# Unit 0's inverse roots on ScalarE and VectorE, its normalising ahead of the low weight parts, its first scores ahead of unit 1's projection

## The chip, the cores and the metric

The kernel runs on one core of a Trainium2 chip. The metric is the device time of one execution in microseconds. Five instruction streams run side by side and meet at semaphores only: TensorE (PE; its weight loads are PEld), VectorE (DVE), ScalarE (ACT), GpSimd (POOL) and the DMA queue of SyncE (SP). Each stream is executed in the order in which it is written: an instruction that waits holds back all that stand behind it on its engine.

## The reference

Four residual blocks on x of shape (4, 256, 256), each on a layer norm of x: a WKV recurrence with the context as values, a quantised dense layer with ReLU, a grouped-query attention with fp8 rounding (self attention and attention to the context), and a small linear attention. The change lies in the third, whose core is:

```
ln_out = _ln(hidden_states, ln_w, ln_b)
q  = _fp8_linear_pertensor(ln_out, wq,  wq_scale,  q_in_scale)   # 16 heads of 128
k  = _fp8_linear_pertensor(ln_out, wk,  wk_scale,  k_in_scale)   # 8 groups
v  = _fp8_linear_pertensor(ln_out, wv,  wv_scale,  v_in_scale)
qx = _fp8_linear_pertensor(ln_out, wqx, wqx_scale, qx_in_scale)
kx, vx = split(einsum('bsi,oi->bso', cond, w_kv_x))
q, k, qx, kx = _ln(...) of each, over its 128 columns
core = softmax(q k^T / sqrt(128)) v ;  xout = softmax(qx kx^T / sqrt(128)) vx
x = x + fp8(cat(core, xout) / smooth) @ wproj^T * scale
```

## The kernel before

The attention is cut into 32 units (`UNITS`): unit u is one group (two query heads) of one of the four batch rows, 256 rows in two halves t = 0, 1. For each unit `project` computes 1024 columns per half in float32 and bf16 parts into PSUM banks `QB[0..3]`; ScalarE takes the sums of squares (`squares`), GpSimd turns them into inverse roots `rs` by a power (`powers`), VectorE multiplies by them (`normalise`), PE transposes the result (`turn`), ScalarE evacuates it with the norm's weights (`evacuate`), PE computes a bf16 copy of the scores (`guard`), VectorE takes its row maxima `nm` (`maxima`), GpSimd spreads them on a diagonal `diag` (`diagonals`), and PE adds that diagonal to the scores (`scores`), of which ScalarE takes the exponentials (`exps`); `weigh` multiplies by the values. The weights of the eight groups are prepared once: for group g, PE turns four blocks (`weights(g, n)`), ScalarE writes their high part, VectorE the low one (`low_weights`), and GpSimd splits the remainder of the third block again (`narrow_parts`).

The order on each engine is written out by hand. The head of the kernel (the first 70 us) runs batch row 0 through the first two blocks and prepares the weights of groups 0 to 3; then a loop over the units sets a fixed order. The change lies at the end of the head, between the last fp8 step of batch row 0 (`fp8(0, (3,))`, VectorE) and the start of the loop. Lines in the trace: the low parts are L1703, the normalising L1720 and L1722, the transposes of `turn` L663, the `guard` L677, the maxima L1730, the diagonal L1332, the scores L691 and L692, the projections L591 and L598, the layer norm statistics L1460, L1463 and L1465, its application L1470, `narrow_parts` L1323 and L1325, the constants `cs` (cosines and sines for the last block, 32 one-column memsets) L1361 and L1362.

A bank of PSUM that PE wants to write again is guarded by `free(o)`, which waits for the bank's last reader. Two of them matter here. Bank XB (bank 7) holds first `turn_h(1)`, the transposed layer norm of batch row 1, which ScalarE's `turned_h(1)` (L999) reads, and then `weights(3, 3)`. Bank SB[0] (bank 4) holds first `weights(3, 0)`, read by `low_weights(3, 0)`, and then the first scores.

## Time and profile before

| quantity | us |
|---|---|
| median of 3 runs | 690.91 (690.83 to 692.33) |
| profiled execution, its own time | 692.9 |
| span of the profile, first to last instruction | 691.1 |
| TensorE busy | 617.9 (89% of the span) |
| VectorE busy | 530.1 (77%) |
| ScalarE busy | 401.0 (58%) |
| GpSimd busy | 254.0 (37%) |

The profile is one execution; its time lies 1.8 us above its span and 2.0 us above the median of the timed runs, so that differences are taken within it and then laid on the median. Starts are counted from the first instruction. In a timeline a row of several instructions (x4) gives the start of the first and the time until the last has ended; neighbouring instructions of one engine overlap a little at their ends. What stands in brackets is the idle time before the row and who ended it.

### The profile page before, as it was taken

The page shows a single profiled execution, that of the slowest core. Times are in us where ns is not written, and L with a number is a line of the kernel's source. Part 1 is how long each engine was busy: PE and PEld are TensorE (multiplying, and loading weights), DVE is VectorE, ACT ScalarE, POOL GpSimd, SP SyncE. Part 2 cuts the span into 40 slices and gives each one's busy share as a digit, 9 for nine tenths or more (in the row PEclk, how much of TensorE's full clock was granted, in tenths as well). Part 3 has the DMA queues.
Part 4 walks back from the last instruction along what each step waited for, and adds up shares of the span by engine and source line. Part 5 has one row for each costly group of instructions (what it writes and reads, how often), then busy time and mean ns, then how long its engine had stood idle before and what let it go on. Part 6 is the DMA issues. An engine that isn't in the chain of part 4 may idle for free.

```text
span 691.1 us, 13273 instructions
## 1 busy us (share of the span) xinstructions
PE 617.9 (89%) x4567; PEld 490.6 (71%) x4567; DVE 530.1 (77%) x1285; ACT 401.0 (58%) x1339; POOL 254.0 (37%) x338
## 2 busy tenths in 40 slices
PE   4446989999989999999899999999999999999936
PEld 3235767766767877877688778877788778877725
DVE  6997778979676757888787568797763776769698
ACT  4255756656777736556757365667563566653531
POOL 2215564444223543334235533332322254421233
PEclk9998999999999999999999999999999999999978
DMA  8236443443483223223243333223342223010001
GB/s 271 73 147 222 138 115 69 153 158 80 146 280 115 76 90 100 100 100 100 100 115 100 100 100 100 100 101 100 100 160 100 98 102 101 16 32 1 1 0 62
DMA packets 36972, 72.86 MB, mean 105 GB/s; under 512 B 3342, under 2 KB 28586, under 8 KB 32810
## 3 DMA queue, kind: packets, MB, share of 16 engines
q1 hardware_dynamic: 36720, 72.00, 32.4%
q8 instruction: 37, 0.61, 0.4%
q14 instruction: 29, 0.24, 0.1%
q10 hardware_dynamic: 186, 0.02, 0.0%
HBM read 59.41 MB, written 12.60 MB: 104 GB/s over the span
## 4 chain that ended last, share of the span: by engine, by line
PE 65%; DVE 22%; ACT 5%; issue 4%; POOL 2%; DMA 1%; SPq 0%; DVEq 0%; ACTq 0%
PE bank L711 14%; PE bank L591 12%; PE bank L691 11%; PE bank L598 7%; PE bank L663 5%; PE bank L735 3%; PE bank L677 3%; PE bank L692 3%; DVE Cb L1745 2%; PE bank L725 1%; POOL rs L1317 1%; PE bank L750 1%; PE bank L481 1%; DVE Cb L1760 1%; DVE rest L1703 1%
## 5 line engine op out<-in xcount | busy, mean ns | idle before, releaser
L711 PEld LDWEIGHTS bank<-V,Pt 128*128 128x128 f32 x1024 | 128.0, 192 | 37.5 <-DVE Cb L1745 26.1
L711 PE MATMUL bank<-V,Pt 128*128 128x129 f32 x1024 | 138.2, 278 | 9.4 <-DVE Cb L1745 9.3
L1069 ACT ACTIVATE square<-bank 128x128 bf16<-128x128 f32 x372 | 98.1, 275 | 78.4 <-PE bank L591 50.8
L1332 POOL TENSOR_TENSOR diag<-identb,nm 128x512 bf16<-128x512 bf16 x64 | 67.1, 1048 | 198.9 <-DVE nm L1730 198.8
L691 PE MATMUL bank<-QT,KTt 128*128 128x512 f32 x256 | 132.7, 600 | 2.4 <-POOL diag L1332 2.4
L1052 ACT ACTIVATE Pt<-bank 128x512 f32<-128x512 f32 x128 | 76.7, 599 | 77.6 <-PE bank L692 74.1
L1730 DVE TENSOR_REDUCE nm<-bank 128x2 f32<-128x512 f32 x128 | 82.0, 682 | 32.5 <-PE bank L677 32.4
L1317 POOL TENSOR_TENSOR rs<-ve,mhalf 128x6 f32<-128x6 f32 x64 | 88.9, 1389 | 5.3
L1743 DVE RECIPROCAL ro<-bank 128x2 f32<-128x2 f32 x128 | 21.3, 166 | 83.3 <-PE bank L711 82.7
L1745 DVE SCALAR_TENSOR_TENSOR Cb<-bank,ro,ism 128x128 bf16<-128x128 f32 x256 | 78.1, 347 | 4.5
L591 PE MATMUL bank<-WQ,xq 128*128 128x256 f32 x512 | 79.7, 298 | 1.8 <-DVE xq L1641 1.5
L591 PEld LDWEIGHTS bank<-WQ,xq 128*128 128x128 f32 x512 | 67.4, 189 | 14.0 <-issue 6.9
L1069 ACT ACTIVATION_READ_ACCUMULATOR square<-bank 128x1 f32 x372 | 76.0, 204 | 0.0
L598 PE MATMUL bank<-WC,vT 128*128 128x256 f32 x256 | 70.6, 400 | 0.0
L1315 POOL TENSOR_SCALAR ve<-ss 128x6 f32<-128x6 f32 x64 | 18.4, 288 | 128.6 <-ACT square L1069 128.6
L1093 ACT ACTIVATE QT<-bank,vec 128x512 f32<-128x512 f32 x64 | 49.9, 780 | 22.6 <-PE bank L663 22.5
L591 PE MATMUL bank<-WH,xh 128*128 128x128 bf16 x768 | 54.0, 220 | 1.5 <-DVE xh L1641 1.5
L691 PEld LDWEIGHTS bank<-QT,KTt 128*128 128x128 f32 x256 | 43.1, 190 | 17.1 <-issue 13.8
L1720 DVE TENSOR_TENSOR Qn<-bank,rs 128x512 f32<-128x512 f32 x64 | 43.8, 684 | 13.4 <-POOL rs L1317 13.4
L663 PE MATMUL bank<-ident,Qn 128*128 128x128 f32 x384 | 48.8, 278 | 2.4 <-DVE Qn L1722 2.4
L1101 ACT ACTIVATE catT<-bank 128x1024 bf16<-128x1024 bf16 x32 | 32.8, 1024 | 27.7 <-PE bank L725 27.7
L692 PE MATMUL bank<-diag,onesb 128*128 128x512 bf16 x128 | 48.5, 379 | 0.0
(233 smaller groups left out, 1030.7 us busy)
## 6 DMA issues: line engine op xcount, KB each, us to landing
WQ<-wq_split SPq DMA_DIRECT2D x24, 1024.0 KB, 7.8
WH<-wh_split SPq DMA_DIRECT2D x24, 384.0 KB, 9.0
wq_split<-WQ SPq DMA_DIRECT2D x8, 1024.0 KB, 4.4
ism<-smooth_inverse SPq DMA_DIRECT2D x32, 256.0 KB, 6.4
wst<-in_L_xattn_wproj SPq DMA_DIRECT2D x16, 256.0 KB, 4.0
wh_split<-WH SPq DMA_DIRECT2D x8, 384.0 KB, 3.8
wst<-in_L_xattn_wq SPq DMA_DIRECT2D x8, 256.0 KB, 5.2
wst<-in_L_xattn_wqx SPq DMA_DIRECT2D x8, 256.0 KB, 5.2
```

The lines of the kernel that those rows point to most:

```text
L591: last = nc.tensor.matmul(o[:, o0:o0 + n], x, w, start=m == 0, stop=m == parts * KT - 1)
L598: last = nc.tensor.matmul(QB[2 * t + 1][:, 2 * P:4 * P], vT[b % 2][:, k, t * P:(t + 1) * P], WC[:, k, g, :], start=k == 0, stop=k == KT - 1)
L663: last = nc.tensor.transpose(o[:, (j * NT + t) * P:(j * NT + t + 1) * P], Qn[:, t, h, :], ident[:])
L691: nc.tensor.matmul(o[:], KTt[u % 2][:, x, t * P:(t + 1) * P], QT[u % 2][:, x, :], start=True, stop=False)
L692: nc.tensor.matmul(o[:], onesb[:], diag[u % 2][:, x].rearrange("p a b -> p (a b)"), start=False, stop=True).then_inc(s["st_done"], 1)
L711: last = nc.tensor.matmul(o[:, h * (P + 2):h * (P + 2) + P + 1], Pt[:, x, k, h * S + t * P:h * S + (t + 1) * P], V[u % 2][:, x, k, 0:P + 1 ...
L1052: A(Pt[:, x, t], SB[n % 2][:], ACT.Exp, scale=SCALE).then_inc(s["exp_done"], 1)
L1069: last = A(square[:, t, h], head(t, h), ACT.Square, accum_out=ss[:, t, h:h + 1])
L1317: gp.tensor_tensor(rs[:, t, :], ve[:, t, :], mhalf[:, 0:6], ALU.pow).then_inc(s["rs_ready"], 1)
L1332: gp.tensor_tensor(diag[u % 2][:, x], identb[:].unsqueeze(1).to_broadcast([P, HPG * NT, P]), nm[u % 2][:, x].rearrange("p h t -> p (h t)") ...
L1730: v.tensor_reduce(nm[u % 2][:, x, :, t], GUARD_BANK[t][:].rearrange("p (h t) -> p h t", h=HPG), AX_X, ALU.max, negate=True).then_inc(s["ma ...
L1745: last = v.scalar_tensor_tensor(out=c4[:, t, x, h, :], in0=o[:, h * (P + 2):h * (P + 2) + P], scalar=ro[:, x, t, h:h + 1], in1=ism[:, u % ...
```

## The change

Five edits, all in the head:

1. The inverse roots of unit 0. Before, GpSimd computed them with `powers(0, 0)` and `powers(0, 1)`. Now ScalarE takes a square root (scale 1/128, bias EPS) over both halves at once behind its last square, and VectorE a reciprocal. Around it two one-element activations on a new tile `table` load ScalarE's function tables: one for the square root before `turned_z(0)`, one for the exponential behind the values. ScalarE's `values(0, 0)` moves ahead of the squares of the second half.
2. VectorE: reciprocal and `normalise(0, *)` move ahead of the three `low_weights(2, *)` and of batch row 1's layer norm statistics; `middle(1, 0)` (L1470, whose result `turn_h(1)` turns) moves behind all four maxima of unit 0.
3. TensorE: `turn(0)` moves ahead of `weights(3, 0)` and `weights(3, 1)`; the first scores of unit 0 move from the start of the loop to behind `guard(0, 1)`; `turn_h(1)` moves behind those scores.
4. ScalarE: the first exponentials move ahead of `weights(3, 2)`, and `turned_h(1)` behind it.
5. GpSimd: the 32 memsets of `cs` move ahead of `narrow_parts(1)`; `norm(1, 0)` moves behind `narrow_parts(2)`.

```diff
--- before.py
+++ after.py
@@ -93,6 +93,8 @@
         lnm = sb("lnm", [P, 3, NT, 2])
         lnst = sb("lnst", [P, NT, 6])
         mhalf = sb("mhalf", [P, 16])
+        epsb = sb("epsb", [P, 1])
+        table = sb("table", [P, 1])
         cs = sb("cs", [P, B, 2, DK3 // 2])
         st3 = sb("st3", [P, T8, 6])
         mv3 = sb("mv3", [P, T8, 2])
@@ -300,7 +302,7 @@
 
             "xq_ready xqT_done xqT_evac ffn_done ffn_read zT_done lnT_evac y4_ready xq4_ready "
 
-            "qkv_done q1_done v_ready ss_ready rs_ready norm_done tr_done qt_evac smax_done "
+            "qkv_done q1_done v_ready ss_ready root_ready rs_ready norm_done tr_done qt_evac smax_done "
             "max_ready diag_ready st_done exp_done pv_done o_evac cq_ready cT2_done catT_evac proj_done x3_ready "
 
             "ve3_ready pw3_ready h3_ready h3T_done h3T_evac conv_ready silu_ready proj3_done qkv3_evac rotated dl_ready "
@@ -775,13 +777,14 @@
             for n in range(3):
                 weights(2, n, HEAD_BANK[2][n])
             project_first()
+            turn(0)
             weights(3, 0, HEAD_BANK[3][0])
             weights(3, 1, HEAD_BANK[3][1])
-            turn(0)
-            turn_h(1)
             guard(0, 0)
             weights(3, 2, HEAD_BANK[3][2])
             guard(0, 1)
+            scores(0, 0, 0)
+            turn_h(1)
             weights(3, 3, HEAD_BANK[3][3])
             project(1, 0)
 
@@ -879,7 +882,8 @@
             for u in range(UNITS - 1):
                 b, g = divmod(u, G)
                 nb, step = ahead(u) or (None, None)
-                scores(u, 0, 0)
+                if u:
+                    scores(u, 0, 0)
                 if u >= SCORES_FIRST:
                     scores(u, 0, 1)
                 if (u + 1) % G == 0:
@@ -1080,8 +1084,12 @@
                     for h in range(4, 6):
                         last = A(square[:, t, h], head(t, h), ACT.Square, accum_out=ss[:, t, h:h + 1])
                     last.then_inc(s["ss_ready"], 1)
-                for t in range(NT):
-                    values(0, t)
+                    if t == 0:
+                        values(0, t)
+                act.wait_ge(s["ss_ready"], NT)
+                A(ve[:], ss[:], ACT.Sqrt, scale=1.0 / P, bias=epsb[:]).then_inc(s["root_ready"], 1)
+                values(0, 1)
+                A(table[:], epsb[:], ACT.Exp)
 
             def evacuate(u, which=range(4)):
 
@@ -1117,6 +1125,8 @@
                 weights(1, n, HEAD_BANK[1][n])
             turned_xq(0)
             weights(2, 3, HEAD_BANK[2][3])
+            act.wait_ge(s["consts_ready"], 1)
+            A(table[:], epsb[:], ACT.Sqrt)
             turned_z(0)
             over_scales(0, range(4))
             for n in range(3):
@@ -1124,9 +1134,11 @@
             first_squares()
             evacuate(0)
             weights(3, 0, HEAD_BANK[3][0])
+            weights(3, 1, HEAD_BANK[3][1])
+            exps(0, 0, 0)
+            weights(3, 2, HEAD_BANK[3][2])
             turned_h(1)
-            for n in range(1, 4):
-                weights(3, n, HEAD_BANK[3][n])
+            weights(3, 3, HEAD_BANK[3][3])
             squares(1, 0)
             values(1, 0)
 
@@ -1164,7 +1176,8 @@
 
             for u in range(UNITS - 1):
                 nb, step = ahead(u) or (None, None)
-                exps(u, 0, 0)
+                if u:
+                    exps(u, 0, 0)
                 if u >= SCORES_FIRST:
                     exps(u, 0, 1)
                 if step == 7:
@@ -1260,6 +1273,7 @@
             chain.add(gp.affine_select(out=ident[:], in_=ident[:], compare_op=ALU.not_equal, fill=1.0, base=0,
                                        pattern=[[-1, P]], channel_multiplier=1))
             chain.add(gp.memset(mhalf[:], -0.5))
+            chain.add(gp.memset(epsb[:], EPS))
             for i in range(2):
                 chain.add(gp.memset(V[i][:, :, :, P:P + 1], 1.0))
             chain.add(gp.memset(OX[:, :, 0:1], NEG_INF))
@@ -1347,12 +1361,6 @@
             norm(0, 1)
             norm(0, 2)
             narrow_parts(0)
-            pool.wait_ge(s["xq4_ready"], 4)
-            narrow_parts(1)
-            powers(0, 0)
-            powers(0, 1)
-            norm(1, 0)
-            narrow_parts(2)
 
             inv_freq = (1.0 / np.float32(10000.0) ** (np.arange(0, DK3, 2, dtype=np.float32) / np.float32(DK3))).astype(np.float32)
             for l in range(B):
@@ -1361,6 +1369,11 @@
                     chain.add(gp.memset(cs[:, l, 0, j:j + 1], float(np.cos(ang))))
                     chain.add(gp.memset(cs[:, l, 1, j:j + 1], float(np.sin(ang))))
             chain.wait()
+
+            pool.wait_ge(s["xq4_ready"], 4)
+            narrow_parts(1)
+            narrow_parts(2)
+            norm(1, 0)
 
             half3 = DK3 // 2
 
@@ -1796,17 +1809,19 @@
                 low_weights(1, n, HEAD_BANK[1][n])
             for p in range(4):
                 fp8(0, (p,))
+            dve.wait_ge(s["root_ready"], 1)
+            v.reciprocal(rs[:], ve[:]).then_inc(s["rs_ready"], NT)
+            normalise(0, 0)
+            normalise(0, 1)
             for n in range(3):
                 low_weights(2, n, HEAD_BANK[2][n])
             early(1, 0)
-            normalise(0, 0)
-            normalise(0, 1)
-            middle(1, 0)
             maxima(0, 0, 0)
             maxima(0, 0, 1)
             low_weights(3, 0, HEAD_BANK[3][0])
             maxima(0, 1, 0)
             maxima(0, 1, 1)
+            middle(1, 0)
             low_weights(3, 1, HEAD_BANK[3][1])
             low_weights(3, 2, HEAD_BANK[3][2])
```

On TensorE, from the second `guard` of unit 0 to unit 1's projection; bank 7 is XB, bank 4 is SB[0]. Before:

```order
L677 MATMUL bank2<-KTt0,QT0 128x256 x2
L677 MATMUL bank3<-KTt0,QT0 128x256 x2
L562 MATMUL bank7<-cen,wst1 128x128
L564 MATMUL bank7<-ident,wst1 128x128
L562 MATMUL bank7<-cen,wst1 128x128
L564 MATMUL bank7<-ident,wst1 128x128
L591 MATMUL bank0<-WQ1,xq0 128x256 x8
L591 MATMUL bank1<-WH1,xh0 128x128 x12
L598 MATMUL bank1<-WC,vT0 128x256 x2
L691 MATMUL bank4<-QT0,KTt0 128x512
L692 MATMUL bank4<-diag0,onesb 128x512
```

Now, the same stretch of the changed kernel:

```order
L679 MATMUL bank2<-KTt0,QT0 128x256 x2
L679 MATMUL bank3<-KTt0,QT0 128x256 x2
L693 MATMUL bank4<-QT0,KTt0 128x512
L694 MATMUL bank4<-diag0,onesb 128x512
L483 MATMUL bank7<-ident,tmp 128x128 x4
L564 MATMUL bank7<-cen,wst1 128x128
L566 MATMUL bank7<-ident,wst1 128x128
L564 MATMUL bank7<-cen,wst1 128x128
L566 MATMUL bank7<-ident,wst1 128x128
L593 MATMUL bank0<-WQ1,xq0 128x256 x8
L593 MATMUL bank1<-WH1,xh0 128x128 x12
L600 MATMUL bank1<-WC,vT0 128x256 x2
```

The scores and the four transposes of `turn_h(1)` (L481 before, ahead of the first `guard`) now stand between the second `guard` and the last weight block, which uses the same bank as those transposes.

On ScalarE, from the evacuation of unit 0 to the last weight block of group 3. Before:

```order
L1093 ACTIVATE QT0<-bank0,vec 128x512
L1035 ACTIVATE WQ0<-bank4,vec 128x256 x2
L999 ACTIVATE tmp<-bank7 128x2x256
L1035 ACTIVATE WQ0<-bank5,vec 128x256 x2
L1035 ACTIVATE WH0<-bank6,vec 128x128 x4
L1039 ACTIVATE WC<-bank7 128x2x256
```

Now:

```order
L1101 ACTIVATE QT0<-bank0,vec 128x512
L1039 ACTIVATE WQ0<-bank4,vec 128x256 x2
L1039 ACTIVATE WQ0<-bank5,vec 128x256 x2
L1056 ACTIVATE Pt<-bank4 128x512
L1039 ACTIVATE WH0<-bank6,vec 128x128 x4
L1003 ACTIVATE tmp<-bank7 128x2x256
L1043 ACTIVATE WC<-bank7 128x2x256
```

The read of bank 7 (`tmp<-bank7`) has moved behind the first exponentials (`Pt<-bank4`) and the four parts of the third block.

On VectorE, behind the last fp8 step. Before:

```order
L1703 SCALAR_TENSOR_TENSOR WQ2<-bank4,vec,WQ2 128x256 x2
L1703 SCALAR_TENSOR_TENSOR WQ2<-bank6,vec,WQ2 128x256 x2
L1703 SCALAR_TENSOR_TENSOR rest<-bank5,vec,WH2 128x128 x4
L1460 BN_STATS lnst<-xs 128x6 x2
L1463 BN_AGGR lnm<-lnst 128x2 x2
L1465 TENSOR_SCALAR lnv<-lnm 128x2
L1720 TENSOR_TENSOR Qn<-bank0,rs 128x512
L1722 TENSOR_TENSOR Qn<-bank1,rs 128x256
L1720 TENSOR_TENSOR Qn<-bank2,rs 128x512
L1722 TENSOR_TENSOR Qn<-bank3,rs 128x256
L1470 TENSOR_SCALAR tmp<-xs,lnm,lnr 128x256 x2
L1730 TENSOR_REDUCE nm0<-bank2 128x2
```

Now:

```order
L1813 RECIPROCAL rs<-ve 128x12
L1733 TENSOR_TENSOR Qn<-bank0,rs 128x512
L1735 TENSOR_TENSOR Qn<-bank1,rs 128x256
L1733 TENSOR_TENSOR Qn<-bank2,rs 128x512
L1735 TENSOR_TENSOR Qn<-bank3,rs 128x256
L1716 SCALAR_TENSOR_TENSOR WQ2<-bank4,vec,WQ2 128x256 x2
L1716 SCALAR_TENSOR_TENSOR WQ2<-bank6,vec,WQ2 128x256 x2
L1716 SCALAR_TENSOR_TENSOR rest<-bank5,vec,WH2 128x128 x4
L1473 BN_STATS lnst<-xs 128x6 x2
L1476 BN_AGGR lnm<-lnst 128x2 x2
L1478 TENSOR_SCALAR lnv<-lnm 128x2
L1743 TENSOR_REDUCE nm0<-bank2 128x2
```

The normalising has moved to the front, so that the low parts and the statistics now stand directly ahead of the first maximum; the application of the layer norm (L1470) is gone from this stretch.

## Rows read from the trace of the kernel before

**Rows 1.** The page: shares of the chain of waits by engine.
```profile
PE 65%; DVE 22%; ACT 5%; issue 4%; POOL 2%; DMA 1%; SPq 0%; DVEq 0%; ACTq 0%
```

**Rows 2.** Chain of waits, 54 to 71 us: start, length, engine, tile, line.
```profile
54.44 1.12 DVE rest L1703 x4
...
58.63 2.82 PE bank L663 x12
...
62.64 1.30 DVE nm L1730 x2
...
65.05 1.64 PE bank L591 x20
...
67.61 0.86 PE bank L691 x2
...
68.69 1.63 PE bank L591 x20
```

**Rows 3.** Timeline of ScalarE, 53 to 73 us: start, length, line, operation.
```profile
53.95 0.22 ACT L1081 ACTIVATION_READ_ACCUMULATOR square<-bank 128x1 f32 x1
54.05 0.67 ACT L1059 ACTIVATE V<-bank 128x256 f32<-128x256 f32 x2
...
62.92 0.62 ACT L999 ACTIVATE tmp<-bank 128x512 f32<-128x512 f32 x1
...
64.11 1.19 ACT L1035 ACTIVATE WH<-bank,vec 128x128 bf16<-128x128 f32 x4
...
72.79 0.60 ACT L1052 ACTIVATE Pt<-bank 128x512 f32<-128x512 f32 x1
```

**Rows 4.** The square root in the tail, line L1240, ScalarE.
```profile
L1240 ACT ACT_TABLE_LOAD  x1: 1283/1283/1283, 670.5 to 670.5; - x1
L1240 ACT ACTIVATE r<-m x1: 283/283/283, 671.8 to 671.8; 128x96 f32<-128x96 f32 x1
```

**Rows 5.** Timeline of VectorE, 41 to 61 us.
```profile
41.56 0.60 DVE L1685 TENSOR_TENSOR vec<-vec 128x1 f32<-128x1 f32 x1
...
52.35 1.65 DVE L1703 SCALAR_TENSOR_TENSOR WQ<-bank,vec,WQ 128x256 fp32r<-128x256 f32 x4
...
56.54 0.17 DVE L1465 TENSOR_SCALAR lnv<-lnm 128x2 f32<-128x2 f32 x1
56.62 0.69 DVE L1720 TENSOR_TENSOR Qn<-bank,rs 128x512 f32<-128x512 f32 x1
...
58.81 2.22 DVE L1470 TENSOR_SCALAR tmp<-xs,lnm,lnr 128x256 f32<-128x256 f32 x1
```

**Rows 6.** Timeline of GpSimd, 58 to 66 us.
```profile
58.81 1.16 POOL L1325 TENSOR_TENSOR WH<-rest,WH 128x512 bf16<-128x512 f32 x1
59.91 0.10 POOL L1361 MEMSET cs<- 128x1 f32 x1
...
64.08 1.04 POOL L1332 TENSOR_TENSOR diag<-identb,nm 128x512 bf16<-128x512 bf16 x1 [3.19 <-DVE nm L1730]
```

**Rows 7.** VectorE, then GpSimd, at 170 to 172 us.
```profile
171.07 0.62 DVE L1465 TENSOR_SCALAR lnv<-lnm 128x2 f32<-128x2 f32 x1
...
170.51 1.15 POOL L1325 TENSOR_TENSOR WH<-rest,WH 128x512 bf16<-128x512 f32 x1
```

**Rows 8.** Windows: length, busy time of each engine, PEclk, DMA share, GB/s.
```profile
48.00:50.00 2.00, 1.23 (x10) 1.01 (x8) 1.86 (x6) 1.40 (x8) 0.00 (x0) 1.00 0.07 21
...
55.50:56.00 0.50, 0.38 (x4) 0.34 (x4) 0.50 (x3) 0.00 (x0) 0.50 (x2) 0.51 1.05 369
...
62.25:62.50 0.25, 0.25 (x4) 0.17 (x2) 0.00 (x0) 0.25 (x2) 0.00 (x0) 0.82 0.91 332
```

**Rows 9.** VectorE at 77 to 96 us.
```profile
77.62 1.93 DVE L1540 SCALAR_TENSOR_TENSOR tmp<-tmp,vec 128x256 f32<-128x256 f32 x2
...
91.82 2.59 DVE L1505 TENSOR_TENSOR_SCAN tmp<-tmp 128x256 f32<-128x256 f32 x2
94.33 1.24 DVE L1508 TENSOR_TENSOR_SCAN tmp<-tmp 128x256 f32<-128x256 f32 x2
```

## The prediction

> **What bounds the kernel.** I read the page first. TensorE is busy 89% of the span (the table above) and holds 65% of the chain that ended last, VectorE 22% [rows 1]: the kernel is a TensorE kernel with stretches in which VectorE sets the pace. The change touches 15 us of it, so I read the chain of waits there next [rows 2]. It runs through VectorE's low parts of group 2 (L1703, the last of them from 54.44) and the layer norm statistics to the normalising, over TensorE's transposes of unit 0 (58.63), `turn_h(1)` and the first guard to the first maxima (62.64, two in 1.30), and from 65.05 on it is TensorE alone: unit 1's projection of half 0 until 67.61 (2.56), the first scores until 68.69 (1.08), and there the projection of half 1. Everything later hangs on that last start. I call it S, and T the start of the transposes (58.63), M the start of the first maximum (62.64). What the change is worth is the shift of S. Then I read the timelines of the other engines for what would be late next, and TensorE's granted clock.
>
> **What it takes away.** The roots: no longer four GpSimd instructions, but one square root and one reciprocal. The last accumulator of the squares is read at 53.95 + 0.22 = 54.17 [rows 3]. A value copy now stands ahead of it (half of the 0.67 for two, 0.34), so 54.51. The square root takes at most the 0.28 of the tail's 96-column one [rows 4]; with 0.05 for a handoff (the chain's gaps are 0.02 to 0.05) it is ready at 54.84. Reciprocal about 0.17 (L1465, as small, takes that) and a handoff: normalising starts at 55.1. Its four instructions began at 56.62 [rows 5] and TensorE could start at 58.63, 2.0 later, so T = 57.1, 1.5 earlier. VectorE stands idle for it from the end of the last fp8 step (the low parts started at 52.35 [rows 5]) to 54.9; those 2.5 us of low parts come behind.
>
> The table loads (1.28 each [rows 4]) cost nothing: the first lies where ScalarE waits for batch row 0's third layer norm, the second between the value copies (end about 55.2) and the first evacuation, which needs transposes and so comes after T: 2 us free at least.
>
> **From T to M.** Before, M = T + 4.01, with the four float32 transposes of `turn_h(1)` ahead of the guard; now two weight blocks stand there instead, 8 bf16 products, about as long (0.38 busy in 0.50 for four at the low clock [rows 8]). TensorE and ScalarE would thus allow M = 61.1. VectorE is later: behind normalising (57.0) come the low parts of group 2, 1.65 [rows 5] and 1.12 [rows 2] less overlap, until about R = 59.7, then the statistics, whose last instruction L1465 starts 0.98 later (54.44 + 1.12 = 55.56 to 56.54 [rows 2, 5]), at 60.7. At R GpSimd starts `narrow_parts(2)`: its cast and, from about R + 0.8, the 1.16 us subtraction L1325 [rows 6], 60.5 to 61.65. A row shows what this does: at 171.07 the same L1465 took 0.62 instead of 0.17 and ended at 171.69, when the L1325 that had begun at 170.51 ended (171.66) [rows 7]. So I take L1465 to be held to 61.7, and M = 61.7: 0.94 earlier than before, not 1.5. Bounds: not held 61.1, or all of L1325 late by one cast more, 62.1.
>
> **From M to S.** This is where the change loses. Before, S = M + 6.05, and the stretch M to 65.05 was short since `turn_h(1)` and the read of its bank were long over. Now the written order makes one chain of five engines' steps:
> - both maxima, 1.30 [rows 2], then the diagonal: before it started at M + 1.44 and took 1.04 [rows 6], so scores can start at M + 2.5. TensorE has nothing else once the guard's second part is over, near M + 1.75 (it needs the second maximum, M + 1.3).
> - scores 0.86 + 0.22 plus the end of the last product, and then the exponential: M + 3.8, 0.60 long [rows 3].
> - ScalarE then writes the third block's four high parts (1.19), and only then reads XB (0.62) [rows 3]. With the usual overlap of 0.1 at each join: M + 6.0. The application of the layer norm, now behind the fourth maximum (1.30, a low part of 0.8, 1.30: M + 3.3), is done at M + 4.0 and its transposes at M + 4.6: not late for this.
> - TensorE's last weight block waits in `free(XB)` for that read, then runs about 0.65 (the second guard ended at 64.4, the projection began at 65.05): unit 1's projection starts at M + 6.7 instead of M + 2.4.
> - 2.56 later, S = M + 9.25. Scores are no longer in between: 1.08 given back, and counted.
>
> S = 61.7 + 9.25 = 70.95 against 68.69: 2.25 later.
>
> **The rest at nothing.** From S on order and partners are the same on all engines, and the steps of unit 1 hang on its projection (roots, normalising), so all shifts together. The scores' early end gives nothing: TensorE is busy from S on without them. SyncE's store of group 2's weights waits for the low parts, 4 us later now, and the loads of group 4 stand behind it in the queue; they were issued by 63.1 before and are first used near 77, so over 5 us stay. GpSimd's memsets take 1.0 us, and the wait for the fp8 step behind them leaves over 9 us to the last of them. L1470, which took 2.22 instead of 0.40, ran in a stretch where VectorE waited for M anyway: its cure is worth nothing.
>
> The moved memsets need a bound. They now follow directly on the L1325 of `narrow_parts(0)`, to whose end VectorE's L1685 was held (0.60 from 41.56, to 42.16, for a single column) [rows 5]. Where memsets followed L1325, L1470 was held to their end: 58.81 + 2.22 = 61.03, with L1325 over at 59.97 and 32 memsets in the 1.0 us from 59.91 [rows 5, 6]. If L1685 fares like that, the whole chain behind it is 0.93 later. Between 0 and 0.93 I take 0: L1685 is another kind of instruction, and it was let go as L1325 ended. The Trainium skill says so too (SBUF — State Buffer, "Who interferes with whom"): an instruction of VectorE with two SBUF inputs is in conflict only with a GpSimd instruction that reads SBUF, and one in a two-port mode, as tensor_scalar can be, with any. By that rule the term is 0; by the row of L1470 taken for all it is 0.93. No run here yet shows a two-input instruction beside a memset.
>
> **Sum.** Span 691.1 + 2.25 = 693.35; the profiled execution 692.9 + 2.25 = 695.15, which lies 2.0 above the median of the runs. On the median: 690.91 + 2.25 = 693.2.
>
> **Rivals.**
> - L1465 is not held (M = 61.1): S 1.65 later, 692.6. For it: at 56.54 it ran in 0.17 beside GpSimd's power; against it: the pair at 171.
> - The clock falls a second time. It fell at 55.5, after TensorE had stood from 53.7, and came back near 62.3, 3.7 us after T [rows 8]. TensorE is now idle from M + 1.75 to M + 2.5, M + 3.6 to M + 4.0 and M + 4.5 to M + 6.0. Against it: from 48 to 50 it was busy for 1.23 of 2.00 us and the clock stayed at 1.00 [rows 8]. If it falls, 3.7 us of projection at half speed cost 1.8: 695.0.
> - The memsets hold L1685: 2.25 + 0.93, 694.1.
> - Not slower, or faster: the delay is given back in the units 0 and 1. VectorE's pairs L1540 and L1505 took 1.93 and 2.59, where L1508, of the same size, took 1.24 [rows 9]; both lay beside work of GpSimd, both on the chain. If the shorter way from unit 1's projection to S moves GpSimd's work past both, 0.69 + 1.35 = 2.0 come back; with L1465 free as well that is 1.65 - 2.0, 690.5. It decides from 1.65 given back. Against it: both hang on S on either engine.
> - One collision goes, the other stays: 2.25 - 1.35, 691.8, no measurable difference.
>
> **Chances.** Forecast 0.45, L1465 free 0.17, clock 0.12, memsets 0.11, one collision gone 0.09, both gone 0.06. A measurement of this kernel tells 0.2% (1.4 us) from no change, so slower begins at 692.3: the first four cases less 0.05 for near misses, 0.80; same 0.16, from those misses and most of the last two cases; faster (below 689.5) 0.04, where more comes back than I can name. Range 692.1 to 695.1: from below the free L1465 to the fallen clock.
>
> **What would show it.** Right: transposes L665 at about 57.1, the first maximum L1743 near 61.7 with L1478 long (about 0.9 us) beside L1339; scores at M + 2.5 waiting for `diag`; TensorE's L564 on bank 7 waiting for ScalarE's L1003; projection of half 1 near 70.9. Wrong: that start below 68.7, or a shift there which is gone by 100 us. L1698 over 1 us long shows the memset case; a granted clock of 0.5 between 66 and 71 the clock case.

## Result

Slower, as forecast, and by more than forecast. In the runs shared by both kernels the changed kernel took 695.45 us (median of 4, 695.27 to 696.58) and the kernel before 691.62 (median of 4, 690.83 to 692.71); the ratio is 1.0051, with a 95% interval of 1.0039 to 1.0063. The forecast was 693.2, with a range of 692.1 to 695.1: the direction was right, the time lies outside the range.

| quantity | before | changed |
|---|---|---|
| median of the shared runs | 691.62 | 695.45 |
| profiled execution, its own time | 692.9 | 695.27 |
| span of the profile | 691.1 | 693.5 |
| TensorE busy | 617.9 (89%) | 613.9 (89%) |
| GpSimd busy | 254.0 (37%) | 249.9 (36%) |

TensorE's 4.0 us less are no work saved: the changed kernel's trace holds 4520 records of its products, the other 4567.

### The profile page after: what moved, and what is told of

It reads as the page before. It is cut to its first block, busy times and chain, and to the rows that moved or that the text cites. A ratio compares the mean times of both kernels' runs of the same rounds, so it can differ in the third digit from the quotient of the medians.

```text
span 693.5 us, 13229 instructions
## 1 busy us (share of the span) xinstructions
PE 613.9 (89%) x4520; PEld 489.8 (71%) x4567; DVE 529.8 (76%) x1286; ACT 404.3 (58%) x1344; POOL 249.9 (36%) x335
## 4 chain that ended last, share of the span: by engine, by line
PE 61%; DVE 24%; ACT 6%; issue 5%; POOL 3%; another core or an unknown queue 1%; DMA 1%; SPq 0%; DVEq 0%; ACTq 0%
PE bank L713 14%; PE bank L593 12%; PE bank L693 10%; PE bank L600 7%; PE bank L665 5%; PE bank L737 3%; PE bank L679 3%; DVE Cb L1758 2%; POOL rs L1331 2%; PE bank L694 2%; PE bank L727 1%; DVE Cb L1773 1%; DVE Cb L1774 1%; PE bank L752 1%; ACT KTt L1101 1%
## 5 line engine op out<-in xcount | busy, mean ns | idle before, releaser
L1331 POOL TENSOR_TENSOR rs<-ve,mhalf 128x6 f32<-128x6 f32 x62 | 86.5, 1396 | 5.2
L600 PEld LDWEIGHTS bank<-WC,vT 128*128 128x128 f32 x256 | 44.7, 194 | 3.7
```

What stands on the lines that cost most here:

```text
L600: last = nc.tensor.matmul(QB[2 * t + 1][:, 2 * P:4 * P], vT[b % 2][:, k, t * P:(t + 1) * P], WC[:, k, g, :], start=k == 0, stop=k == KT - 1)
L1331: gp.tensor_tensor(rs[:, t, :], ve[:, t, :], mhalf[:, 0:6], ALU.pow).then_inc(s["rs_ready"], 1)
```

## The profile after

TensorE's timeline of the changed kernel, 56 to 74 us (start, length, line, operation; in brackets the idle time before it and who ended it):

```profile
56.59 2.82 PE L665 MATMUL bank<-ident,Qn 128*128 128x128 f32 x12 [3.82 <-DVE Qn L1735]
...
61.81 0.91 PE L679 MATMUL bank<-KTt,QT 128*128 128x256 bf16 x4 [0.47 <-DVE nm L1743]
63.53 1.10 PE L693 MATMUL bank<-QT,KTt 128*128 128x512 f32 x2 [0.81 <-POOL diag L1346]
64.94 0.66 PE L483 MATMUL bank<-ident,tmp 128*128 128x128 f32 x4 [0.32 <-DVE tmp L1483]
67.04 0.49 PE L564 MATMUL bank<-cen,wst 128*128 128x128 f32 x2 [1.44 <-ACT tmp L1003]
...
67.73 1.19 PE L593 MATMUL bank<-WQ,xq 128*128 128x256 f32 x8
...
70.18 1.30 PE L593 MATMUL bank<-WQ,xq 128*128 128x256 f32 x8
```

The transposes start at 56.59 instead of 58.63 [rows 2]. Then the waits that were not there before stand in a row: 0.81 for the diagonal, 0.32 for the layer norm's application, and 1.44 in which the last weight block waits for ScalarE to read its bank. Unit 1's half 1, the last row, starts at 70.18.

ScalarE's timeline of the changed kernel over the same stretch:

```profile
64.88 0.60 ACT L1056 ACTIVATE Pt<-bank 128x512 f32<-128x512 f32 x1 [3.13 <-remote]
65.37 1.13 ACT L1039 ACTIVATE WH<-bank,vec 128x128 bf16<-128x128 f32 x4
66.37 0.62 ACT L1003 ACTIVATE tmp<-bank 128x512 f32<-128x512 f32 x1
```

It stood 3.13 us waiting for the scores ("remote" is a releaser that the profile could not name; in the written order it is TensorE's scores that the exponential waits for), then did the exponential, the third block and the read of XB one after the other, with the last weight block held behind them. Before, that read began at 62.92 [rows 3].

VectorE's timeline of the changed kernel:

```profile
41.01 0.60 DVE L1698 TENSOR_TENSOR vec<-vec 128x1 f32<-128x1 f32 x1
...
54.33 0.23 DVE L1813 RECIPROCAL rs<-ve 128x12 f32<-128x12 f32 x1 [2.46 <-ACT ve L1090]
...
60.11 0.96 DVE L1478 TENSOR_SCALAR lnv<-lnm 128x2 f32<-128x2 f32 x1
60.99 1.27 DVE L1743 TENSOR_REDUCE nm<-bank 128x2 f32<-128x512 f32 x2
...
72.93 0.69 DVE L1733 TENSOR_TENSOR Qn<-bank,rs 128x512 f32<-128x512 f32 x1 [5.27 <-POOL rs L1331]
...
73.87 1.26 DVE L1502 TENSOR_TENSOR_SCAN tmp<-vec,tmp 128x256 f32<-128x256 f32 x2
...
79.46 2.51 DVE L1553 SCALAR_TENSOR_TENSOR tmp<-tmp,vec 128x256 f32<-128x256 f32 x2
```

L1698 (L1685 before) took 0.60 as before, with the 32 memsets now right behind the subtraction that holds it: the memset rival is dead, and this trace agrees with the rule weighed there, of the Trainium skill (SBUF — State Buffer, "Who interferes with whom"), that two SBUF inputs on VectorE don't collide with a GpSimd instruction that only writes. It is one instruction of a single column, so the evidence is thin. L1478 took 0.96 instead of 0.17 [rows 5], as forecast, and ended with GpSimd's subtraction (59.89 to 61.05). The last row is the loss that I had not seen: the pair took 1.93 before [rows 9].

To compare kernels I take four starts in each trace and count from F, the end of the last fp8 step, since all traces agree up to there but for 0.6 us of drift. T, M and S are the starts of unit 0's transposes, of the first maximum and of unit 1's half 1, here all by the rows of the timelines. (The row of S in the kernel before is 68.34; the chain in [rows 2] puts it at 68.69, since neighbouring rows of the timeline overlap and the chain counts from the end of the piece before.) "Pair" is the length of L1540 with its two instructions, L1553 in the changed kernel. P is the start of the second pair (L1505 before, L1518 in the changed kernel), and the last column runs from P to the end of the span.

| kernel | F | T-F | M-T | S-M | S-F | pair | P-S | rest |
|---|---|---|---|---|---|---|---|---|
| before | 52.42 | 6.21 | 4.01 | 5.70 | 15.92 | 1.93 | 23.48 | 599.3 |
| e1 before again | 51.97 | 6.20 | 4.14 | 5.69 | 16.03 | 1.93 | 23.48 | 599.4 |
| changed | 51.87 | 4.72 | 4.40 | 9.19 | 18.31 | 2.51 | 24.05 | 599.3 |
| e3 scores ahead alone | 51.79 | 6.19 | 3.29 | 9.27 | 18.75 | 2.50 | 24.05 | 599.1 |
| e2 scores back | 52.32 | 4.72 | 4.39 | 8.25 | 17.36 | 1.94 | 23.49 | 599.2 |
| e5 third block ahead | 52.07 | 4.72 | 4.40 | 8.43 | 17.55 | 2.51 | 24.06 | 597.8 |
| e8 narrow parts early | 51.92 | 4.73 | 4.39 | 9.19 | 18.31 | 0.94 | 23.40 | 597.8 |
| e6 statistics first | 52.03 | 4.73 | 4.81 | 9.23 | 18.77 | 2.51 | 24.07 | 599.3 |
| e7 roots only | 51.79 | 4.72 | 5.33 | 5.70 | 15.75 | 1.94 | 23.49 | 599.4 |
| e10 kept busy | 51.86 | 6.21 | 4.14 | 5.69 | 16.04 | 1.92 | 23.47 | 597.7 |
| e13 first wait filled | 52.01 | 6.21 | 3.39 | 5.69 | 15.29 | 1.93 | 23.48 | 597.9 |
| e11 two fixes | 51.84 | 6.20 | 3.54 | 5.68 | 15.42 | 1.12 | 23.40 | 597.8 |
| e12 roots and fixes | 51.91 | 4.73 | 4.24 | 5.68 | 14.65 | 1.12 | 23.41 | 597.9 |
| e14 scores back, waits filled | 51.98 | 4.72 | 4.40 | 8.26 | 17.38 | 1.95 | 23.50 | 599.5 |

From this table the change costs 2.39 up to S (-1.49 + 0.39 + 3.49) and 0.58 in the pair: 2.97. Both traces have the same 599.3 us from P on. The spans differ by 2.4 only because the changed kernel's trace happens to be 0.55 ahead at F, from a first load that landed after 4.31 instead of 5.00 us.

One column scatters by itself. Up to M the kernels before, e1, e10 and e11 are the same program on TensorE and VectorE, and M-T is 4.01, 4.14, 4.14 and 3.54. It goes with the moment at which TensorE's granted clock comes back to 2.4 GHz: behind M in e1 and e10, 0.3 us ahead of M in the kernel before, 0.8 us ahead in e11. The window from 61 to 62 us shows e10 at half clock and e11 at full clock (length, busy times of PE, PEld, DVE, ACT and POOL, granted clock, DMA share, GB/s):

```profile
61.00:62.00 1.00, 1.00 (x7) 0.80 (x6) 0.00 (x0) 1.00 (x3) 0.00 (x0) 0.50 0.99 366
```

```profile
61.00:62.00 1.00, 0.99 (x11) 0.73 (x9) 0.42 (x1) 1.00 (x4) 0.00 (x0) 1.00 1.06 336
```

So a single trace of that kernel is uncertain by 0.6 us at S. In the changed kernel, e2, e5, e8 and e14 the clock came back anywhere from 1.6 us ahead of M to 1.5 us behind it, and M-T stayed 4.39 or 4.40: there VectorE sets M.

## Experiments

Each experiment was timed against the kernel before in five rounds; ratios are to that kernel.

### The size of the scatter (e1)

The kernel before, without an edit.

> The kernel before, unchanged, against itself. Both theories: no difference (690.8 to 692.7 us). It is for the size of the scatter: the profiled execution of before took 692.9, 2.0 above the lower of its runs, while that of the changed kernel took 695.3, its lowest. If this profile is one of about 690.9, it shows where an execution of before gains or loses those 2 us, and the true distance of the two spans is then nearer 4 than 2.4 us.

Measured: 692.61 us (690.96 to 693.09), the kernel before beside it 692.49, ratio 1.0002 (0.9993 to 1.0010). Its trace repeats the first one (S-F 16.03, pair 1.93). So no profile of the lower value was caught, but the runs settled something else: the 28 executions of these runs lie on two levels: 4 of them at 691.0 to 691.5, 22 at 692.1 to 693.1, and 2 between. The 690.91 on which I had laid my sum was a median of three, two of them on the lower level. Against the usual level, 692.5, the changed kernel's 695.4 is 2.9 more, which is what the table gives.

### One part alone: the first scores ahead, on the kernel before (e3)

```diff
 # TensorE
             turn(0)
-            turn_h(1)
             guard(0, 0)
             weights(3, 2, HEAD_BANK[3][2])
             guard(0, 1)
+            scores(0, 0, 0)
+            turn_h(1)
             weights(3, 3, HEAD_BANK[3][3])
 # ScalarE
             weights(3, 0, HEAD_BANK[3][0])
-            turned_h(1)
             weights(3, 1, HEAD_BANK[3][1])
+            exps(0, 0, 0)
             weights(3, 2, HEAD_BANK[3][2])
+            turned_h(1)
             weights(3, 3, HEAD_BANK[3][3])
 # both: the first scores and exponentials out of the loop
 # VectorE: middle(1, 0) from ahead of the maxima to behind all four
```

> The kernel before, with nothing but the first scores and exponentials put ahead of unit 1's projection, turn_h(1) and its read behind them, and the layer norm's application behind the maxima; roots, low parts and memsets as before. Theory A (the order behind the first maximum is the loss: scores, exponential, third block, read of XB, last weight block, projection): the start of unit 1's half 1 lies 9.5 us behind the first maximum instead of 6.05, so about 3 us slower than before, 694 to 695. Theory B (the loss comes from the roots on ScalarE and VectorE, with the low parts of group 2 late): as before within 0.7 us.

Measured: 695.85 us (694.22 to 697.26), ratio 1.0049 (1.0037 to 1.0061), the whole loss of the change. S-M is 9.27 against 5.70 before. Its TensorE timeline has the same wait ahead of the last weight block:

```profile
67.41 0.49 PE L562 MATMUL bank<-cen,wst 128*128 128x128 f32 x2 [1.51 <-ACT tmp L1001]
```

Theory B, in which the roots are the loss, falls. The roots alone are worth 1.49 at T in every kernel that has them.

### That part undone in the changed kernel (e2)

```diff
 # TensorE, ScalarE: scores(0, 0, 0) and exps(0, 0, 0) back at the start of the loop
-            scores(0, 0, 0)
-            exps(0, 0, 0)
 # VectorE
             maxima(0, 0, 1)
+            middle(1, 0)
             low_weights(3, 0, HEAD_BANK[3][0])
             maxima(0, 1, 0)
             maxima(0, 1, 1)
-            middle(1, 0)
```

> The changed kernel with the first scores and exponentials back at the start of the loop; turn_h(1) behind the second guard, the layer norm's application behind the first two maxima; roots, normalising and memsets as in the changed kernel. Theory A: unit 1's half 1 starts about M + 7.6 instead of M + 9.5, so 1.9 us faster than the changed kernel, 691 to 692.5, near before. Theory B: it stays within 0.7 us of the changed kernel (3.5 us over before).

Measured: 696.30 us (693.88 to 697.22), ratio 1.0049 (1.0034 to 1.0064): by the runs, nothing was won. In the trace, an execution of 694.2, S-F fell by 0.95 and the pair by 0.57 to 1.94. S-M was 8.25, not 7.6. The second guard starts 0.82 behind M as in the changed kernel; what is late is the layer norm's application, which now runs beside GpSimd's diagonal (62.78 to 63.92) and takes 1.44 instead of the changed kernel's 0.72:

```profile
62.63 1.44 DVE L1479 TENSOR_SCALAR tmp<-xs,lnm,lnr 128x256 f32<-128x256 f32 x2
```

Behind its end, 2.64 after M, the transposes, the read and the last weight block still stand in a chain. The prediction of the trace was half right and that of the time wrong: four of six executions lay 1.6 to 3 us above the profiled one. The later experiment with filled waits is about those.

### ScalarE's order (e5)

```diff
             weights(3, 1, HEAD_BANK[3][1])
-            exps(0, 0, 0)
             weights(3, 2, HEAD_BANK[3][2])
+            exps(0, 0, 0)
             turned_h(1)
```

> The changed kernel with one swap on ScalarE: the four high parts of the third block (1.13 us) ahead of the first exponential, in time in which ScalarE waits for the scores, instead of behind it. Theory A (the read of bank XB behind them holds the last weight block): the read starts 1.0 earlier, then bound by the transposes of turn_h(1); unit 1's half 1 at M + 8.5, 1.0 us faster than the changed kernel. Rival (the scores' wait for the diagonal on TensorE is what costs, ScalarE's order nothing): no change against the changed kernel.

Measured: 694.75 us (693.31 to 695.07), ratio 1.0035 (1.0022 to 1.0048). ScalarE's timeline:

```profile
61.81 1.18 ACT L1039 ACTIVATE WH<-bank,vec 128x128 bf16<-128x128 f32 x4
65.08 0.60 ACT L1056 ACTIVATE Pt<-bank 128x512 f32<-128x512 f32 x1 [2.09 <-remote]
65.83 0.60 ACT L1003 ACTIVATE tmp<-bank 128x512 f32<-128x512 f32 x1 [0.16 <-PE bank L483]
```

The third block now fills a wait, the read of XB starts right behind its transposes, and TensorE's wait for it falls from 1.44 to 0.69; S-M falls by 0.76, where 1.0 had been expected, and the median lies 0.70 below that of the changed kernel. The link between ScalarE's order and the last weight block is shown.

### Where the 0.58 came from (e8)

```diff
-        NARROW_BEHIND = {0: 3, 1: 4, 4: 6, 5: 7}
+        NARROW_BEHIND = {1: 4, 4: 6, 5: 7}
 # GpSimd, loop over the units
                 diagonals(u, 0)
+                if u == 0:
+                    narrow_parts(3)
```

> The changed kernel with GpSimd's narrow_parts(3) (1.8 us) moved from behind unit 1's roots into the 7.9 us in which GpSimd waits for their squares. Theory: VectorE's L1553 was held 0.57 us longer in the changed kernel than before since GpSimd's differences for batch row 1 began later against it; now they begin 1.8 us earlier, and the pair takes 1.0 to 1.4 instead of 2.51: 1.1 to 1.5 us faster than the changed kernel. Rival (the length of L1553 is hidden by another wait): no change.

Measured: 693.25 us (693.05 to 696.84), ratio 1.0028 (1.0017 to 1.0039). S-F is 18.31 as in the changed kernel, to the hundredth, and the pair takes 0.94. But of these 1.57 us only 0.65 arrive at the second pair (P-S 23.40 instead of 24.05). The rest of the 2.2 us by which the median lies below the changed kernel's isn't the pair: this trace has 597.8 us behind P and not 599.3, which is the clock at 98 us (below). Below a pair of about 1.9 us another chain ends last, over ScalarE's evacuations; so the pair is worth the 0.57 that the changed kernel lost in it, and 0.08 more. This kernel's chain of waits, where the changed kernel's has the pair:

```profile
79.01 0.84 ACT WQ L1039 x2
79.86 0.79 ACT tmp L978 x2
```

GpSimd's timeline in the changed kernel shows what had lengthened the pair:

```profile
73.87 0.67 POOL L1329 TENSOR_SCALAR ve<-ss 128x6 f32<-128x6 f32 x1
74.63 1.62 POOL L1331 TENSOR_TENSOR rs<-ve,mhalf 128x6 f32<-128x6 f32 x1
...
78.00 1.04 POOL L1299 TENSOR_TENSOR tmp<-tmp 128x512 f32<-128x512 f32 x1
```

The same instructions in the kernel before, with VectorE's scans first:

```profile
70.94 1.26 DVE L1489 TENSOR_TENSOR_SCAN tmp<-vec,tmp 128x256 f32<-128x256 f32 x2
...
71.99 0.21 POOL L1315 TENSOR_SCALAR ve<-ss 128x6 f32<-128x6 f32 x1 [1.01 <-ACT square L1069]
72.28 1.32 POOL L1317 TENSOR_TENSOR rs<-ve,mhalf 128x6 f32<-128x6 f32 x1
...
75.36 1.04 POOL L1285 TENSOR_TENSOR tmp<-tmp 128x512 f32<-128x512 f32 x1
```

The roots of unit 1's half 1 hang on S. VectorE's scans of batch row 1 (L1502) hang on the roots of half 0, and so on the projection of half 0. Before, the first scores stood between the two projections; now they follow each other directly, and the scans come 1.1 us later against S. They fall on GpSimd's small instructions, which take 0.67 and 1.62 us instead of the 0.21 and 1.32 of the same two before. GpSimd's differences (L1299) start 7.82 behind S instead of 7.02, and hold VectorE's pair. That GpSimd's differences hold the pair is shown by this run; that the scans made them late is read from the traces. All four kernels with the scores ahead and GpSimd's order unchanged have 2.50 or 2.51, and those with the scores in the loop and that order have 1.92 to 1.95.

### The statistics ahead of the low parts (e6)

```diff
 # VectorE
+            early(1, 0)
             for n in range(3):
                 low_weights(2, n, HEAD_BANK[2][n])
-            early(1, 0)
```

> The changed kernel with the layer norm statistics of batch row 1 ahead of the low parts of group 2 instead of behind them. Theory: the statistics' last instruction (0.96 us instead of 0.17) was held by GpSimd's subtraction, which starts behind the low parts; now it takes 0.17, the first maximum starts 0.5 to 0.7 us earlier against the transposes (4.0 behind them), and the kernel is 0.5 us faster than the changed one. Rival (the first maximum waits for the guard anyway): no change.

Measured: 696.50 us (694.49 to 698.01), ratio 1.0064 (1.0048 to 1.0080). A miss. The statistics' last instruction took 0.17 as expected, but M-T rose from 4.40 to 4.81: the low parts now end 1.1 us later, and with them the bank that `weights(3, 1)` needs ahead of the guard. The clock also came back 0.5 us later against T than in the changed kernel, and the guard sets M here; how much of the 0.41 that is, one trace doesn't tell.

```profile
60.50 0.61 PE L558 MATMUL bank<-cenb,wst 128*128 128x128 bf16 x4 [0.49 <-DVE rest L1716]
60.90 0.98 PE L679 MATMUL bank<-KTt,QT 128*128 128x256 bf16 x4
```

So the held L1478 is real, but its removal was not worth anything in this order: VectorE's work behind the normalising is 3.8 us long, and in this order the low parts at its end hold the guard's bank.

### The roots alone (e7)

```diff
 # VectorE
             normalise(0, 1)
+            early(1, 0)
             low_weights(2, 0, HEAD_BANK[2][0])
             low_weights(2, 1, HEAD_BANK[2][1])
+            middle(1, 0)
             low_weights(2, 2, HEAD_BANK[2][2])
 # TensorE: turn(0), turn_h(1), weights(3, 0), guard(0, 0), weights(3, 1), weights(3, 2), guard(0, 1)
 # first scores and exponentials in the loop; ScalarE's turned_h(1) behind weights(3, 0) again;
 # VectorE: early(1, 0) and middle(1, 0) gone from their places in the changed kernel;
 # GpSimd: norm(1, 0) ahead of narrow_parts(2)
```

> The changed kernel's roots, normalising and transposes ahead, but the first scores in the loop as before, the statistics directly behind the normalising, their application ahead of group 2's third low part, and turn_h(1) directly behind the transposes of unit 0. Theory A: the 1.5 us won at the transposes reach unit 1's half 1, which starts 6.0 behind the first maximum again: 1.0 to 1.5 us faster than before, 4 us faster than the changed kernel. Rival (VectorE's low parts of group 2 behind the normalising make the first maximum late): not faster than before by more than 0.5 us.

Measured: 692.21 us (689.78 to 692.66), ratio 0.9995 (0.9987 to 1.0004). No gain. S-M is 5.70 again, as theory A wants, but M-T is 5.33: `turn_h(1)`, directly behind the transposes, waited 0.53 for VectorE and ran at the low clock ahead of the guard. The 1.49 of the roots shrank to 0.17 at S. Here the rival was right by the median; single executions went down to 689.78, and none of those was profiled.

### The two levels: the clock in TensorE's wait at 94 us (e10)

```diff
+                if u == 1:
+                    keep_busy(9)     # 9 products, bf16, 128 by 512, into bank XB
                 weigh(u, 0, 1)
```

> The kernel before with nine extra products (bf16, 128 by 512, into a bank that nobody reads) in the 2.6 us in which TensorE waits for VectorE at 93.8 (unit 1). Theory: the two levels in which executions of one kernel lie, 1.5 us apart (691.1 and 692.6 for before; 693.3 and 694.8 for the changed kernel with the third block ahead, whose one profile without a granted clock of 0.5 at 97 to 100 belongs to the lower), are the clock falling in this wait or not. Then all executions lie on the lower level, 690.9 to 691.3, and the clock is 1.00 between 90 and 105. Rival (the two levels come from elsewhere): both levels stay. If the products run longer than the wait, up to 0.5 us is lost.

Measured: 691.16 us (690.25 to 691.61), ratio 0.9987 (0.9979 to 0.9996); all 11 executions lie within 1.4 us, where those of the kernel before have two levels. Three windows, 98 to 100 us; the columns are the length, the busy times of PE, PEld, DVE, ACT and POOL, the granted clock, the DMA share and GB/s. The kernel before in its second profile, the changed kernel with the third block ahead in its execution of 693.31, and this one:

```profile
98.00:100.00 2.00, 2.00 (x12) 2.00 (x11) 0.02 (x1) 1.25 (x2) 1.97 (x2) 0.50 0.21 23
```

```profile
98.00:100.00 2.00, 1.80 (x16) 1.80 (x17) 1.64 (x6) 0.00 (x0) 2.00 (x3) 1.00 0.00 0
```

```profile
98.00:100.00 2.00, 2.00 (x23) 1.99 (x22) 0.05 (x1) 2.00 (x5) 1.87 (x2) 1.00 0.53 149
```

TensorE waits 2.6 us for VectorE in unit 1; in some executions the clock falls to 1.2 GHz near the end of it and in others it stays at 2.4. All traces sort by this: in eight the clock fell between 94 and 100 us and the rest behind P is 599.1 to 599.5 us; in six it stayed at 1.00 and the rest is 597.7 to 597.9. Three of those six have no extra products in this wait (e5, e8, e13). That is the scatter of 1.5 us, and the reason why a median of three was a poor base. What decides in a single execution whether the clock falls isn't shown. Of the 1.4 us that are left between e10's executions, the scatter of M-T can account for 0.6; the rest is open.

### The wait ahead of the transposes, filled (e13)

```diff
 # TensorE; keep_busy as above, with other operands
             weights(3, 0, HEAD_BANK[3][0])
+            keep_busy(7)
             weights(3, 1, HEAD_BANK[3][1])
+            keep_busy(9)
             turn(0)
```

> The kernel before with 7 + 9 extra products (bf16, 128 by 512, into a bank nobody reads, 3.5 us in all) in the wait between unit 0's projection and its transposes; nothing else. Theory: the wait ahead of the transposes costs twice, once by itself and once by the granted clock of 0.5 that follows it: the twelve transposes take 1.5 instead of 2.8 us and the first maximum starts 1.3 to 1.6 us earlier (61.0, where VectorE's held L1470 ends), so 1.3 us faster than before. Rival (the maximum waits for ScalarE's evacuations and VectorE, whatever the clock): no change.

Measured: 691.39 us (689.72 to 692.57), the kernel before beside it 692.68, ratio 0.998 (0.997 to 0.999).

```profile
58.22 1.53 PE L663 MATMUL bank<-ident,Qn 128*128 128x128 f32 x12 [0.67 <-DVE Qn L1730]
60.69 0.66 PE L481 MATMUL bank<-ident,tmp 128*128 128x128 f32 x4 [0.94 <-DVE tmp L1478]
```

The transposes took 1.53 instead of 2.82, as expected, but only 0.62 arrived at M: `turn_h(1)` then waited 0.94 for the layer norm's application, which GpSimd's memsets held. Against the other traces of the same head it is 0.15 to 0.75, by when the clock came back in them. By this reading the edit that moves the memsets away does have a worth, but only once the clock no longer covers it; no run shows the two together.

### The upper level of the kernel with the scores back (e14)

```diff
 # TensorE, on the kernel with the scores back; 3 + 3 products into bank QB[0]
+            keep_busy(3)
             turn_h(1)
+            keep_busy(3)
             weights(3, 3, HEAD_BANK[3][3])
```

> The kernel with the first scores back in the loop (levels 693.9 and 696.8, its profile of the lower one) with 3 + 3 extra products in TensorE's waits around turn_h(1), before and behind. Theory: its upper level, 2.6 to 3 us above, is the clock falling a further time in these waits, so that unit 1's projection starts at 0.5; filled, all executions lie at 693.9 to 694.6. Rival: the upper level comes from elsewhere and stays, or all executions take it.

Measured: 694.10 us (692.51 to 695.63, 8 executions), ratio 1.0024 (1.0014 to 1.0034), against 696.30 without the six products. The group at 695.8 to 697.2 is gone but for one execution at 695.63, six lie at 693.83 to 694.21, and S-M stayed at 8.26. That fits the clock falling again in the waits between the maximum and unit 1's projection, one of my rivals; no profile fell on such an execution, so it isn't seen directly. For the changed kernel itself, whose four executions lie at 695.3 to 696.6, it wasn't tried.

### Two versions below both kernels (e11, e12)

```diff
 # two fixes, on the kernel before: narrow_parts(3) early (GpSimd), keep_busy(9) in unit 1 (TensorE)
 # roots and fixes: those two, and from the changed kernel roots, normalise and memsets; first scores in the loop;
 # VectorE, ScalarE and GpSimd's norm(1, 0) as in the roots alone;
 # TensorE: turn(0), weights(3, 0), guard(0, 0), turn_h(1), weights(3, 1), weights(3, 2), guard(0, 1)
```

> The kernel before with narrow_parts(3) early on GpSimd (as in the changed kernel with that move, where the pair L1540 fell from 2.51 to 0.94) and the nine extra products at 93.8. Theory: the pair falls from 1.93 to 0.9 to 1.2, 0.8 to 1.0 us on the chain, and the clock stays: 1.0 us faster than the kernel with the nine products alone, 690.2, 2.1 below before. Rival: the pair was not on the way of later work, no gain over the nine products.

> The roots by ScalarE and VectorE, normalising and transposes ahead as in the changed kernel, first scores in the loop as before, turn_h(1) behind the first guard, the statistics directly behind the normalising, and both moves of the kernel with two fixes. Theory: the first maximum starts 4.2 to 4.4 behind the transposes instead of 5.3 with turn_h(1) ahead of the guard, unit 1's half 1 6.0 behind the maximum: 0.9 us faster than the kernel with two fixes, 689.3, 3 below before. Rival (VectorE's low parts, now behind the normalising, set the maximum in every order): no faster than the two fixes alone.

Measured: the two fixes 691.06 us (690.33 to 691.65), ratio 0.9978 (0.9969 to 0.9987), 1.6 below the kernel before beside it, not 2.1. The pair took 1.12, but P-S is 23.40 against 23.47 with the nine products alone, so here the rival was right: this fix is worth 0.07. Roots and fixes 689.78 us (689.59 to 690.05), ratio 0.9959 (0.9947 to 0.9971): 2.9 below before, 5.7 below the 695.45 of the changed kernel. Its TensorE timeline:

```profile
56.64 2.82 PE L665 MATMUL bank<-ident,Qn 128*128 128x128 f32 x12 [3.83 <-DVE Qn L1740]
59.25 0.63 PE L558 MATMUL bank<-cenb,wst 128*128 128x128 bf16 x4
59.68 1.06 PE L679 MATMUL bank<-KTt,QT 128*128 128x256 bf16 x4
60.53 0.67 PE L483 MATMUL bank<-ident,tmp 128*128 128x128 f32 x4
```

From the transposes on there is no wait in it; M-T is 4.24, S-M 5.68. The idea in the change, roots without GpSimd's power and normalising first, gains when `turn_h(1)` stays ahead of the third block: S-F is 14.65 against 15.92 in the kernel before, and against 15.42 and 16.04 in e11 and e10, whose head is the same. So it is 0.8 to 1.4 at S, and 1.28 between the medians of e11 and e12.

## Why the prediction was right in direction and short in size

Three steps failed: the sum was laid on runs of the wrong level (1.6), the units behind S were taken to shift together (0.58), and the last weight block was priced too low (0.29). M itself came 0.16 earlier than forecast. Together that is 2.3, against 2.25 between 693.2 and 695.45.

- Roots, T. Forecast 1.5 earlier; 1.49 against F. Right, by its own steps.
- T to M, with L1465 (now L1478) held to the end of GpSimd's subtraction. Forecast 0.94 earlier in all; 1.10 (-1.49 + 0.39). Right.
- M to S, the chain over diagonal, scores, exponential, third block, read of XB and last weight block. Forecast 3.20 longer; 3.49. Right in every link up to the read, which ended at M + 6.01 where M + 6.0 had been forecast. The 0.29 are the last weight block: priced at 0.65, it took 0.93, since its first two products, behind the wait, took 0.49 instead of 0.22. The chain of the changed kernel, then that of the kernel before:

```profile
67.04 0.49 PE bank L564 x2
...
67.97 1.64 PE bank L593 x20
```

```profile
64.39 0.22 PE bank L562 x2
...
65.05 1.64 PE bank L591 x20
```

  Experiment e3 shows the whole chain alone, e5 shows the link of ScalarE's order.
- Moved memsets at nothing, table loads at nothing. Right; the table load ran from 54.51 to 55.79 and the evacuation began at 57.75.
- "From S on order and partners are the same on all engines, and the steps of unit 1 hang on its projection, so all shifts together." This step failed. Half 0's steps hang on the projection of half 0, half 1's on S, and the change brought the two 1.1 us nearer to each other. It cost 0.58 in the pair of L1553. I had named the same collision as a way in which time might come back, and not asked which way it would move. The price that I gave for its end, 0.69, was wrong too: with the pair at 0.94 or 1.12 only 0.08 comes back against the kernel before. The second pair kept its length, 2.60 against 2.59.
- "On the median: 690.91 + 2.25." This step failed too, and is the larger part of the miss: 692.5, the usual level, is 1.6 above the base that I took. Within the traces the change was 2.25 by the forecast and 2.97 as measured, but the median of three was a draw mostly from the lower of two levels 1.5 us apart, while the profile from which the sum came, at 692.9, was of the upper one. I had seen the two, noted that they lay 2.0 apart, and let it go. Laid on the profiled time, the sum gives 695.15 and the range would have held 695.45.
- The clock falling a further time: not in the changed kernel's trace, where it stood at 1.00 from 66 to 71 us (and from 62 to 96). For its other executions it is open, for the kernel with the scores back made likely.

```profile
66.00:71.00 5.00, 3.96 (x36) 3.81 (x37) 1.13 (x4) 3.16 (x16) 0.00 (x0) 1.00 0.89 303
```

## What to carry over

Before an instruction is pulled ahead, list what stands behind it on its engine and who waits for that: the scores were ready work for an idle moment, but the bank XB was behind them, through three engines. Two chains that hang on different events, here the two halves of one unit, don't shift together when something between the events is moved; look at what they do to each other. Lay a sum only on runs of the level from which the trace comes. And follow a shortened instruction to the next start that hangs on it: the pair lost 1.57 us and the kernel 0.65.

## What the runs showed of the hardware

- A wait of TensorE can cost twice. With 3.82 us of it ahead of the transposes in the changed kernel, and 1.95 + 2.40 in the kernel before, these took 2.82 us at a granted clock of 0.5; with the wait filled by products that nobody reads, 1.53. Behind the 2.6 us wait at 94 us the clock fell in eight traces and not in six, worth about 1.5 us, and nine products in it took the upper level away (all 11 executions at 690.25 to 691.61).
- The moment at which the clock comes back scatters too, and with it the kernel before's M-T, 3.54 to 4.14.
- A row of 32 memsets on GpSimd held a tensor_scalar of VectorE to its end (2.22 us instead of 0.40) but not a tensor_tensor with two SBUF operands: L1698 stayed at 0.60, held only by the subtraction ahead of them.
- A GpSimd instruction with two inputs over 512 columns holds a tensor_scalar of VectorE too: 0.96 instead of 0.17 us beside the subtraction, 1.44 instead of 0.72 beside the diagonal (e2).
- GpSimd's instructions on 6 columns, too, get longer beside VectorE's scans: 0.67 and 1.62 us instead of 0.21 and 1.32.
